# A Mamba-2 scan on one core: the stage ahead merged into the scan's steps, and decay blocks laid out for two engines

## The reference, cut to what matters

```python
proj = hidden_states @ W_in.T                  # z 4096, xBC 4096+2*128, dt 64 columns
xBC = silu(causal_conv4(xBC) + conv_b)         # x, B, C; convolution per channel and sequence
dt = softplus(dt + dt_bias); A = -exp(A_log)   # 64 heads of 64 channels
# per head, chunks of 32 tokens: Y_diag = (C B^T * exp(segsum(dt*A))) (x*dt), and the state between chunks
y = (Y_diag + Y_off) + D_param * x
g = y * silu(z)
gn = g * rsqrt(mean(g*g) + EPS) * norm_w
return gn @ W_out.T
```

## Time and profile before

| | |
|---|---|
| median of 3 runs | 1691.82 us (1690.84 to 1691.88) |
| span of the profiled execution | 1691.9 us |
| stage ahead of the scan | 0 to about 90 us |
| scan | about 90 to 952 us |
| cross attention and experts | the rest |

### The profile page before, as it was taken

The page is one execution under the profiler, slowest core; times in us unless marked ns, Lnnn a source line. Parts: engine busy times, 40 slices in busy tenths (PEclk is TensorE's granted clock), DMA queues, the critical chain, the costliest instruction groups (busy, mean ns, idle before and its releaser), DMA issues. The chain is left out here.

```text
span 1691.9 us, 29098 instructions
## 1 busy us (share of the span) xinstructions
PE 1603.2 (95%) x9864; PEld 1281.0 (76%) x9864; DVE 1254.0 (74%) x2044; ACT 1217.1 (72%) x2518; POOL 731.8 (43%) x601
## 2 busy tenths in 40 slices
PE   5479999999999999999999999999969999999999
PEld 3357777777777777777777677878757889999888
DVE  7969999999999999999999865567666533333355
ACT  4679999999999999999999576566624324444331
POOL 1425555555555555555555511311113653334460
PEclk9689999999999999999999999999989999999999
DMA  8966444444444444444444100000215323222231
GB/s 324 389 231 253 164 152 172 150 158 167 151 172 152 154 171 150 173 151 153 172 150 150 55 1 13 14 14 14 72 75 190 117 96 133 90 91 95 79 99 51
DMA packets 78078, 226.62 MB, mean 134 GB/s; under 512 B 9072, under 2 KB 32880, under 8 KB 76272
## 3 DMA queue, kind: packets, MB, share of 16 engines
q1 hardware_dynamic: 72272, 198.67, 32.9%
q0 software_dynamic: 5664, 26.09, 4.4%
HBM read 187.77 MB, written 36.96 MB: 133 GB/s over the span
## 5 line engine op out<-in xcount | busy, mean ns | idle before, releaser
L776 DVE SCALAR_TENSOR_TENSOR m_xc<-banks,k_cw,m_xc 128x510 f32<-128x510 f32 (+2 forms) x384 | 285.4, 743 | 16.6 <-ACT m_xc L690 7.2
L917 PE MATMUL m_ps_out<-k_won,m_gT 128*128 128x256 f32 x1024 | 242.3, 379 | 3.2 <-POOL m_gT L640 2.0
L873 PE MATMUL banks<-pair_hi,m_wxz 128*128 128x512 f32 x680 | 241.7, 406 | 2.5 <-DMA m_wxz<-w_split 2.5
L640 POOL TENSOR_TENSOR m_gT<-m_gy,m_zs 128x512 f32<-128x512 f32 x128 | 166.4, 1300 | 172.3 <-DVE m_gy L817 171.4
L663 POOL TENSOR_TENSOR m_mat<-m_mat,k_cbm 128x384 f32<-128x384 f32 x128 | 129.8, 1014 | 230.6 <-DVE m_mat L789 216.8
L917 PEld LDWEIGHTS m_ps_out<-k_won,m_gT 128*128 128x128 f32 x1024 | 193.6, 190 | 36.1 <-POOL m_gT L640 3.3
L905 PE MATMUL m_ps_y<-m_mat,m_xdt 128*64 128x256 f32 (+1 forms) x2048 | 194.7, 332 | 0.0
L711 ACT ACTIVATE m_mat<-m_mat 128x1536 f32<-128x1536 f32 x128 | 188.6, 1473 | 0.0
L905 PEld LDWEIGHTS m_ps_y<-m_mat,m_xdt 128*64 128x64 f32 x2048 | 126.8, 136 | 80.0 <-issue 42.3
L702 ACT ACTIVATE m_mat<-m_a_all,k_cum 128x256 f32<-128x256 f32 x340 | 170.6, 502 | 0.0
L651 POOL TENSOR_TENSOR m_g_sum<-m_g_sum,m_g_sq 128x512 f32<-128x512 f32 x124 | 162.4, 1310 | 5.3 <-ACT m_g_sq L717 5.1
(11 more groups left out here) (325 smaller groups left out, 3774.9 us busy)
## 6 DMA issues: line engine op xcount, KB each, us to landing
m_wxz<-w_split SPq DMA_DIRECT2D x85, 512.0 KB, 3.4
m_a_all<-a_by_head SPq DMA_DIRECT2D x85, 512.0 KB, 4.4
k_w_first<-w_split SPq DMA_DIRECT2D x43, 512.0 KB, 3.3
k_a_first<-a_by_head SPq DMA_DIRECT2D x43, 512.0 KB, 4.2
w_split<-p_w_hl SPq DMA_DIRECT2D x15, 1024.0 KB, 8.6
raw<-in_w_gate_up POOLq DMA_DIRECT2D x9, 1280.0 KB, 6.5
raw<-in_w_xz SPq DMA_DIRECT2D x16, 512.0 KB, 7.1
raw<-in_w_down POOLq DMA_DIRECT2D x9, 640.0 KB, 7.9
```

Of the source, the lines that this page charges most:

```text
L640: pool.tensor_tensor(gT[:, n % 2, :], gy[:, n % 2, :], zs[:, n % 2, :], ALU.mult).then_inc(g_done, 1)
L776: dve.scalar_tensor_tensor(out=out[:, :, k:], in0=ps[:, :, 0:SEQ - k], scalar=cw[:, c, TAPS - 1 - k:TAPS - k], in1=out[:, :, k:], op0=ALU. ...
L873: last = pe.matmul(ps[:, :], w, a, start=m == 0, stop=m == len(terms) - 1)
L917: last = pe.matmul(ps_out[:, q * HID:(q + 1) * HID], gT[:, n % 2, q * P:(q + 1) * P], won[:, c, :], start=c == 0 and q % 2 == 0, stop=c == ...
```

## The change

`mamba_prepare` and `mamba_scan` become one function, `mamba_phase`. Ahead of the scan only group 0 is prepared (tiles 0 to 7 are turned, the second half of them for group 1). Groups 1 to 3 are prepared inside the scan: `prepare_next(n)` on TensorE, ScalarE and VectorE adds, at fixed steps j of group g, one piece of the work of group g+1 (and the tiles of group g+2). dt, cum and C times B are kept for two groups; the softplus works on 256 columns at a time. In the scan the taps of B and C are read from a copy in SBUF (`bc_copy`), not from PSUM.

W_in is split tile by tile in group 0, into the buffer that the step itself uses, and stored from there for groups 1 to 3: three tiles on ScalarE and GpSimd ahead, the other 29 on GpSimd alone (`w_high`, `w_low`). Half of W_out is scaled by GpSimd in steps 0 to 15 (`weigh_out`). GpSimd normalises the tiles of groups 2 and 3.

A step's decay matrices are laid out as 1024 columns of diagonal blocks (masked), then 512 columns of the blocks beside them (not masked). VectorE multiplies the first in one instruction, GpSimd the second, both with C times B broadcast over the two heads. ScalarE's 256 column `gaps` and TensorE's 256 column operand now lie in two pieces of 128.

The loads for cross attention move from step 8 to step 98. The diff, cut to its core (in the order: layout, SyncE, GpSimd, ScalarE, VectorE, TensorE):

```diff
+        def diagonal(u):
+            return mat[:, u, 0:2 * HPT * BG * P].rearrange("p (h c) -> p h c", h=HPT)
+
+        def beside(u):
+            return mat[:, u, 2 * HPT * BG * P:].rearrange("p (h c) -> p h c", h=HPT)
+
+        def first_rows(u, h, b):
+            at = (h * BG + b) * 2 * P
+            pair = mat[:, u, at:].rearrange("p (j t) -> p j t", t=P)
+            step = (2 * HPT * BG * P + (h * BG + b) * P - at) // P
+            return pair[:, 0:step + 1:step, :]
+
+        def later_rows(u, h, b):
+            at = (h * BG + b) * 2 * P + P
+            return mat[:, u, at:at + P]
...
+            def w_store(c):
+                sp.wait_ge(w_lo_done, c + 1)
+                sp.dma_start(w_dram[c], wxz[c % 3].rearrange("p s w k m -> p (s w k m)").bitcast(F32))\
+                    .then_inc(w_stored[c % 3], 16)
+                if c + RING < NCT:
+                    raw_load(c + RING)
...
+            for c in range(AHEAD):
+                w_store(c)
+            x_load(2)
+            a_store(0)
+            for n in range(3):
+                a_load(n)
+            wo_load(1)
+            x_load(3)
+            for k in range(-2, N):
+                g, j = k // NCT, k % NCT
+                if k + 5 < N:
+                    a_load(k + 5)
+                if AHEAD <= k + 4 < NCT:
+                    w_store(k + 4)
+                elif NCT <= k + 4 < N:
+                    w_load(k + 4)
+                if j == 24 and 0 <= g < NG - 1:
+                    a_store(g + 1)
+                if k == (NG - 1) * NCT + 2:
+                    sp.wait_ge(w_lo_done, NCT)
+                    sp.wait_ge(a_stored, 32 * NG)
+                    sp.wait_ge(cb_done, BG * NG)
                     for dst, src, loaded in next_loads:
                         sp.dma_start(dst, src).then_inc(loaded, 16)
...
+            def w_high(c):
+                pool.wait_ge(raw_loaded[c % RING], 16 * (c // RING + 1))
+                pool.wait_ge(z_ready, c - 2)
+                pool.wait_ge(w_stored[c % 3], 16 * (c // 3))
+                pool.tensor_copy(part(c, 0), w_raw[:, c % RING]).then_inc(w_hi_pool, 1)
+
+            def w_low(c):
+                if c < AHEAD:
+                    pool.wait_ge(w_hi_act, c + 1)
+                else:
+                    pool.wait_ge(w_hi_pool, c - AHEAD + 1)
+                pool.tensor_tensor(part(c, 1), w_raw[:, c % RING], part(c, 0).bitcast(F32), ALU.subtract)\
+                    .then_inc(w_lo_done, 1)
+
+            def weigh_out(c):
+                if c == WO_ACT:
+                    pool.wait_ge(wo_loaded[1], 16)
+                    pool.wait_ge(late_loaded, 16 * (1 + HPT))
+                pool.tensor_scalar(won[:, c, :], won[:, c, :], nw[:, c:c + 1], None, ALU.mult).then_inc(won_pool, 1)
+
+            def matrices_off(n):
+                g, off = n // NCT % 2, beside(n % 3)
+                pool.wait_ge(exp_done, n + 1)
+                pool.wait_ge(cb_done, (n // NCT + 1) * BG)
+                pool.tensor_tensor(off, off, cb_off[:, g * BG:(g + 1) * BG, :].rearrange("p b t -> p (b t)").unsqueeze(1)
+                                   .broadcast_to([P, HPT, BG * P]), ALU.mult).then_inc(mat_off, 1)
+
...
-            pool.wait_ge(w_stored[2], 16 * (NCT // 8))
-            def last_matrix(n):
-                pool.wait_ge(exp_done, n + 1)
-                pool.tensor_tensor(mat[:, n % 3, 1, TRI:2 * TRI], mat[:, n % 3, 1, TRI:2 * TRI],
-                                   cbm[:, n // NCT * BG + 1, :], ALU.mult).then_inc(mat_last, 1)
-
-            last_matrix(0)
+            consts()
+            ln_root(0)
+            ln_root(1)
+            small_low()
+            for c in range(AHEAD):
+                w_low(c)
+            w_high(AHEAD)
+            w_low(AHEAD)
+            matrices_off(0)
             for n in range(N):
-                if n % NCT == 1 and n > 1:
-                    root(n // NCT - 1)
+                g, j = n // NCT, n % NCT
+                if j == 1 and n > 1:
+                    root(g - 1)
                 if n + 1 < N:
-                    pool.wait_ge(mat_done, HPT * (n + 2))
-                    last_matrix(n + 1)
+                    pool.wait_ge(mat_done, n + 2)
+                    matrices_off(n + 1)
+                if n + 4 < NCT:
+                    w_high(n + 4)
+                    w_low(n + 4)
                 if n < N - 1:
                     product(n)
                 if n % NCT > 0:
...
+                if n < NCT - WO_ACT:
+                    weigh_out(WO_ACT + n)
+                if g < NG - 2:
+                    if j == 5:
+                        ln_root(g + 2)
+                    if 7 <= j < 7 + TPG:
+                        normalise((g + 2) * TPG + j - 7)
...
-                    t = g * TPG + 2 * b
-                    act.activation(mat[:, u, h, b * TRI:b * TRI + SEQ], a_all[u][:, h, b * SEQ:(b + 1) * SEQ],
+                    t = g % 2 * TPG + 2 * b
+                    act.activation(first_rows(u, h, b),
+                                   a_all[u][:, h, b * SEQ:(b + 1) * SEQ].rearrange("p (j t) -> p j t", t=P),
                                    ACT.Relu, bias=cum[:, t, head:head + 1], scale=-1.0)
-                    last = act.activation(mat[:, u, h, b * TRI + SEQ:(b + 1) * TRI],
-                                          a_all[u][:, h, b * SEQ + P:(b + 1) * SEQ],
...
+            def prepare_next(n):
+                h, j = n // NCT + 1, n % NCT
+                if j == 3:
+                    bc_scale(h, 0)
+                if j == 4:
+                    bc_copy(h, 0)
+                if j == 6:
+                    bc_scale(h, 1)
+                if j == 7:
+                    bc_copy(h, 1)
+                if j == 8:
+                    bc_tanh_of(h, 0)
+                if j == 9:
+                    dtT_copy(h)
+                if j == 11:
+                    bc_tanh_of(h, 1)
+                if j == 13:
+                    soft_exp(h)
+                if j in (14, 28) and h + 1 < NG:
+                    for n in range(2):
+                        xT_high((h + 1) * TPG + n + (2 if j == 28 else 0))
+                if j == 24:
+                    aT_copy(h)
...
             def matrices(n):
-                g, u = n // NCT, n % 3
+                g, diag = n // NCT % 2, diagonal(n % 3)
                 dve.wait_ge(exp_done, n + 1)
-                dve.tensor_tensor(mat[:, u, 0, :], mat[:, u, 0, :],
-                                  cbm[:, g * BG:(g + 1) * BG, :].rearrange("p b t -> p (b t)"), ALU.mult)\
-                    .then_inc(mat_done, 1)
-                dve.tensor_tensor(mat[:, u, 1, 0:TRI], mat[:, u, 1, 0:TRI], cbm[:, g * BG, :], ALU.mult)\
-                    .then_inc(mat_done, 1)
+                if n % NCT == 0:
+                    dve.wait_ge(cb_done, (n // NCT + 1) * BG)
+                dve.tensor_tensor(diag, diag, cb_diag[:, g * BG:(g + 1) * BG, :].rearrange("p b t -> p (b t)").unsqueeze(1)
+                                  .broadcast_to([P, HPT, BG * 2 * P]), ALU.mult).then_inc(mat_done, 1)
 
             def silu_x(n):
...
+            def prepare_next(n):
+                h, j = n // NCT + 1, n % NCT
+                if h + 1 < NG:
+                    if j < TPG:
+                        tile_stats((h + 1) * TPG + j)
+                    if j == 4:
+                        tile_aggr(h + 1)
+                    if j in (15, 16, 29, 30):
+                        xT_low((h + 1) * TPG + {15: 0, 16: 1, 29: 2, 30: 3}[j])
+                if 5 <= j < 5 + CONV:
+                    bc_taps_of(h, 0, j - 4)
+                if 8 <= j < 8 + CONV:
+                    bc_taps_of(h, 1, j - 7)
+                if j == 11:
+                    bc_silu(h, 0)
+                if j == 12:
+                    soft_begin(h)
+                if j == 13:
+                    bc_silu(h, 1)
+                if j == 14:
+                    soft_first(h)
+                    soft_step(LOG1P[-2])
+                if 15 <= j < 19:
+                    for c in LOG1P[-3 - 2 * (j - 15):-5 - 2 * (j - 15):-1]:
+                        soft_step(c)
+                if j == 19:
+                    soft_end(h)
+                if j == 20:
+                    masked(h, 0)
+                if j == 22:
+                    cum_copy(h)
+                if j == 26:
+                    masked(h, 1)
+
...
+            normalise(4)
+            normalise(5)
+            soft_begin(0)
+            normalise(6)
+            normalise(7)
+            soft_first(0)
+            for c in LOG1P[-2::-1]:
+                soft_step(c)
+            dve.wait_ge(a_neg, 1)
+            soft_end(0)
+            xT_low(4)
+            xT_low(5)
+            cum_copy(0)
+            for k in range(1, TAPS):
+                bc_taps_of(0, 0, k)
+            xT_low(6)
+            xT_low(7)
+            for k in range(1, TAPS):
+                bc_taps_of(0, 1, k)
+            bc_silu(0, 0)
+            bc_silu(0, 1)
```

(51 more changed lines are left out.)

907 lines of the change are left out of this document (431 added, 476 removed).

## The result

The changed kernel takes 1676.64 us (median of 4 runs, 1675.88 to 1679.63) against 1691.65 us: a ratio of 0.9909, 95% interval 0.9896 to 0.9921. It is 15.0 us faster; the two profiled executions are 17.0 us apart. The forecast was 1685.0, so the sign was right and the gain about twice the size.

A forecast was written before the change was run, and what follows sets the result against it. TensorE was taken to bound the scan, waits for chains of other engines the stage ahead. Start -53.8, group 0 +29.5, groups 1 and 2 +17.0 sum to -7.3 us: 1685 us from 1691.9, range 1663 to 1704.

The forecast's parts named there:

- The start: Stage ahead of the scan: only group 0 prepared, so the third scan group starts at 67.0 instead of 120.8 us, -53.8 us.
- the lock: Shared SBUF port: GpSimd's work and VectorE's two-SBUF-operand instructions wait each other out and add up, 7.43 us in steps to 15.
- Group 0: First 32 scan steps: GpSimd becomes the bound, its work and VectorE's two-SBUF-operand work add up, +29.5 us.
- 10.1: VectorE in steps 5 to 19: six taps, two silu and 13 softplus operations priced at 10.1 us together.
- The upper bound of +36: Group 0's cost with GpSimd's scaling at 0.82 us and each hand-off between GpSimd and VectorE doubled: +36 us.
- The moved work in groups 1 and 2: Scan of groups 1 and 2, preparing groups 2 and 3: TensorE is full, so added work counts in full, +17.0 us.
- from there a step takes 6.57 us: Scan from its third matmul group on: one step takes 6.57 us, bound by TensorE; group 3 was forecast to keep this.
- Group 3: Last group of the scan: steps stay 6.57 us, and loads moved from step 8 to 98 cost nothing, 0 us.
- A: Whole kernel: the forecast itself with its spread from start and prices, 1677 to 1695 us, chance 0.45.
- B: Group 0: GpSimd keeps up, so only TensorE's 9 us are paid there, 1664 us in all, chance 0.2.
- C: Steps 2 to 27: waits of VectorE, TensorE and GpSimd run in a ring, 17 us, 1702 us in all, chance 0.2.
- D: ScalarE bounds all along, its writes to two blocks of 128 costing 0.1 us more: +20 us, 1705 us, chance 0.08.

The follow-up runs named there:

- without the trip: Changed kernel, the first three loads of running sums read rows of x instead of waiting for the store to DRAM and load back: 1677.3 us.
- the kernel with the 64 bytes: Changed kernel with an unused tile of 64 bytes per partition ahead of the three buffers of projection weights: 1682.24 us.
- the kernel before in the fast place: Kernel before with an unused tile of 448 bytes per partition ahead of its projection weight buffers: 1686.59 us, ratio 0.9959 to the kernel before.
- the tile behind the weights: Changed kernel with the unused 64 bytes per partition allocated behind the three buffers of projection weights: 1676.29 us.
- the order was changed: GpSimd's gated product moved ahead of the weights' low part: 1685.64 us on the changed kernel, 1676.49 us with W_out's scaling also on ScalarE.
- the kernel with the scaling on ScalarE: Changed kernel with 29 of 32 W_out tiles scaled by ScalarE ahead of the scan, three by GpSimd: 1670.22 us.

## Why the forecast was right, and where not

**The start, -53.8, measured -53.7.** Right in size, by luck in part, and mostly right in its links: dt projection from 15.27 us (forecast 14.6), fold ended at about 20.1 (20.5), dA ready at about 28.9 (28.2). The softplus steps were dearer in the lock (nine took 6.02 us). What was not seen is that ScalarE's scaling of W_out ends at 39.18 us, where the trip through DRAM was forecast to end; without the trip the start was the same. That the two ends fall on the same 39 us is luck.

**Group 0, +29.5, measured +24.5.** The mechanism was right: the lock's sign is in the rows, and taking the second SBUF operand away from one VectorE instruction gives 9.9 us back, the slow clock that hung on the waits included. The terms were off in both directions. The scaling was priced at 0.5 us, within bounds of 0.31 and 0.82; it costs 0.93, outside them, because I leaned on a copy's row. Leaving it out gave 7.2 us. (The Trainium skill's "GPSIMD Engine Reference", section 3.1, has a best case of about 1.8 cycles per element at 1.2 GHz, by which 256 columns are an estimate of 0.38 us; the measured 0.93 decides.) On the other side the sum let each step pay in full from step 2 on; steps 2 and 3 cost nothing (6.52 us each); no run tested why, and it would fit that a late GpSimd first uses up the room between its product and TensorE's need. And of the "10.1" only a part came: the six taps were priced 0.77 us over each, but in the rows only the first of each convolution waited (1.64 us against 0.74), and the softplus steps wait 0.30 us each. Not in the sum at all was the clock: in two steps with a wait of over 3 us the next matmuls ran at half speed, 4.7 us. The upper bound of +36 was added up too low as well: with the scaling at 0.82 and 0.18 more per hand-off, 29.5 + 14 x 0.32 + 26 x 0.18 is 38.7. The Trainium skill's rule that the forecast leaned on ("SBUF — State Buffer", Who interferes with whom) is borne out: the instruction with one SBUF input runs beside GpSimd at its own 1.21 us, the one with two doesn't.

**The moved work in groups 1 and 2, +17.0, measured +12.2.** Set beside the kernel with the 64 bytes, whose weights lie as before's in speed (220.3 and 218.3 us), it is 8.5 + 6.5 = 15.0 against 8.9 + 8.1. So TensorE's additions were sized well, 2.0 us too high, and the rest of the difference is the place. Group 2's 6.5 us are the 6.6 of its matmuls alone: the 1 us for broken overlaps of weight loads, which had no row, and the 0.5 for VectorE didn't show there. Group 1's 8.5 leave 1.1 beyond its matmuls' 7.4.

**The place of the weights, 0 in the forecast, -4.2 to -5.6 in the runs.** This is the step that failed: "from there a step takes 6.57 us" was carried over to a kernel with other places. With the 64 bytes the span is 1680.5 us, and the change gains 11.4 us of 1691.9: start -52.6, group 0 +24.4, groups 1 and 2 +15.0, group 3 +1.7, the rest +0.1. Against the kernel before in the fast place it gains 1 - 0.9909 / 0.9959 = 0.5%, some 8 us. The forecast's -7.3 was of this effect, whose size by these runs is 8 to 11. In group 0 the place is worth nothing (24.5 and 24.4; 23.2 with the tile behind the weights), which fits, since GpSimd sets the steps there.

**Group 3, 0, measured +0.4.** It is two things. The loads for cross attention that moved to step 98 stall step 100 (8.49 us), as they stalled step 6 before (8.19): in both steps TensorE waits for the split weights (1.7 and 1.4 us), which are issued behind them. These 2.0 us were forecast as nothing, and so was the loss of the old stall from group 0. The place gives 1.4 of them back.

**The rivals.** A's range (1677 to 1695) has the measured 1676.6 just outside its lower end. B (1664) is 12.6 off, and its reason is wrong: GpSimd doesn't keep up. C was not there, as argued, until the order was changed. D was wrong: ScalarE's 256 column write to two pieces takes 0.50 us as before.

## What to carry over

When work is moved to an engine that is half idle, price it by its own form of instruction, and look at which of its instructions will then lie beside two-operand instructions of the engine that shares its port: here the same scaling was almost free on ScalarE ahead of the scan (third scan group at 67.41 for 67.05 us) and cost 7 us on GpSimd inside it. An in-order queue is full before it is 100% busy, and moving an instruction to its consumer's convenience can cost more than its own length if it makes the engine wait at the queue's head. And before a small difference is put down to a change, undo the places of buffers: an unused tile of 64 bytes was worth a quarter to a third of this one's gain.

## What the runs showed of the hardware

- Where a matmul's weights lie in SBUF changes its rate: projection matmuls of 128x512 start 0.230 us apart in the mean in one place and 0.233 to 0.234 in two others (28 and 64 bytes on), in the changed kernel at 700 to 900 us with a granted clock of 1.00. Twelve of them are 2.84 or 2.89 us. Why is open.
- GpSimd's multiply of 128x256 by a per-partition scalar takes 0.93 us alone, more than its own two-input subtraction of 128x256 at 0.819 and half again its copy of 128x512 at 0.61. The same form with two scalars (normalisation) took 1.2 to 2.2 us in the scan.
- TensorE, which had idled 3.09 us, came back at a granted clock of 0.53, close to the lower of its two levels (1.2 of 2.4 GHz), and ran eight output matmuls in 3.68 us. After idling 3.47 us it took 3.78 us for them, and 2.54 for the 16 scan matmuls behind. After idling 1.48 us, in the kernel with the scaling on ScalarE, the same eight took 1.99 us:

```profile
141.55 1.99 PE L1058 MATMUL m_ps_out<-m_won,m_gT 128*128 128x256 f32 x8 [1.48 <-POOL m_gT L393]
```

- The lock is between instructions, not engines: VectorE's reduction of 1024 columns (1.21 us, GpSimd 91% busy), and its taps with one operand in PSUM (three in 2.29 us, GpSimd 92% busy), ran at full speed beside GpSimd.
